# A one-core attention and feed-forward kernel: the one-hot product in two row strips, and half of x2 transposed by VectorE and moved by transfers

## The chip, the core and the metric

The kernel runs on one core of a Trainium2 chip. The core has TensorE (matrix products, two records each here: PEld loads the stationary operand, PE streams the moving one), VectorE (DVE), ScalarE (ACT), GpSimd (POOL), SyncE (SP, which here only issues transfers) and 16 DMA engines that carry out what SP and ACT issue. The metric is the device time of one execution in microseconds; lower is better.

## The reference, cut to what matters

All arithmetic is float32. `x` has 32 batches of 32 rows (channels) by 512 columns, 1024 rows in all.

```python
h  = einsum('bct,bcd->bdt', x, cond_weights[itok])     # 16 matrices of 32x32, one chosen for each batch
q, k, v = h @ Wq + bq, h @ Wk + bk, h @ Wv + bv        # 512 -> 4096, 32 heads of 128; rms_norm of q and k
x2 = x + softmax(q k^T / sqrt(128)) v @ Wo + bo        # attention inside each batch of 32 rows
y  = causal_conv(x2, K) + D * x2, columns >= length masked   # one filter K of 512 taps for each channel
out = x2 + y @ ffn_w + ffn_b + (low-rank terms chosen by a gate)
```

The first line is called the mix below, `x2` is the residual stream after attention, and the fourth line is the convolution.

## The kernel before, in words

The program is one straight list of instructions for each engine; semaphores order them against each other. The order of each list is written out by hand. The 1024 rows are eight groups of 128 rows (four batches of 32). There are four stretches.

**Start (0 to 17 us).** Which of the 16 matrices a batch uses is a one-hot product on TensorE: `onehot` (16 rows that count, the other 112 hold zeros in `cond_nat`) times `cond_nat`, twice 512 columns (L825). VectorE fills the unused rows of `cond_nat` with zeros (L1526, L1527), builds `onehot` (L1533, L1536), and turns the product from PSUM into the block-diagonal `mix_w` in two transposes (L1549). `spin` (L817) is a run of products whose result nobody reads; it stands ahead of the one-hot product and behind it. Then come eight groups of the mix (L839, order MIX_ORDER = 0, 4, 1, 5, 2, 3, 6, 7), which ScalarE and VectorE carry out of PSUM as a high part, a low part and a whole (`mix_hi`, `mix_lo`, `mix_f`). SP loads x in four pieces of two groups each, and the weights of head 0 (`w_raw`) behind the first two pieces.

**Heads and values (17 to 506 us).** Products for 32 heads, then for the values. GpSimd forms sums of weights and of `mix_f` for them, one behind the other, starting with L520.

**Attention and output projection (506 to 744 us).** Eight units; each multiplies into four PSUM banks and VectorE adds these to `acc` (L1840), which becomes x2. Units 6 and 7 finish the groups 0 to 3 and 4 to 7 of x2. In unit 7, TensorE does `project_first(7)`, then the transposes of the finished groups 0 to 3 (`transpose_x2`, L1119, four of 128x128 each), and then `project_second(7, g)` for g = 0 to 3 with the transposes of groups 4 to 7 between and behind them. ScalarE copies each transposed group from PSUM to `x2p` (`x2_out`, L1484). `x2p` is stored as [partition, channel, chunk, batch], so that this copy writes with a stride of 128 elements and a stationary operand of the convolution is 32 elements in a row.

**Convolution and feed-forward (744 us to the end).** `convolve(u)` (L1149) for u = 0 to 7, each 16 products of 32 columns of `x2p` by a strip of `toep`, four of them side by side in the four column strips of the array. `toep0` is loaded by SP at about 723 us, once VectorE has turned `a_turn` and `b_turn` (L1877, L1878); behind it SP sends these through DRAM (`a_scr`, L456, 16 transfers; `b_scr`, L458, 4 transfers) and reads them back as `a_all`, `b_all` (L462 to L466), and loads `fb_rows` (L468). ScalarE needs `b_all` at L1504, in the fourth step of the convolution; TensorE needs `a_all` behind the last.

## Time and profile before

| | us |
|---|---|
| median of 3 runs | 806.17 (805.47 to 806.24) |
| the profiled execution's own time | 805.49 |
| its span | 803.7 |
| PE busy | 795.6 |
| DVE busy | 643.1 |
| POOL busy | 520.5 |
| ACT busy | 332.2 |

Busy time is the sum of an engine's instructions. The chain of waits is followed back from the last instruction to whatever released each step. A timeline row gives the start, the time that the row's instructions span, engine, line, operation, tiles and how many instructions are merged; in brackets stands how long the engine had been idle and what released it. SPq and ACTq are rows of issued transfers. A row by stretch gives the stretch, its length, busy time and count of PE, PEld, DVE, ACT and POOL, the granted clock (1.00 is full), the mean busy share of the 16 DMA engines, and GB/s. A product in float32 shows as two PE records for each matmul.

### The profile page before, as it was taken

The numbers are of one execution on the slowest core, as the hardware profiler recorded it, in microseconds if no ns is written. First come the engines' busy times: TensorE is split into PE (matmuls) and PEld (weight loads), VectorE is DVE, ScalarE is ACT, GpSimd is POOL, SyncE is SP. The second block draws the span as 40 slices with busy tenths as digits, with TensorE's granted clock in tenths as the row PEclk, the third lists the DMA queues.
The fourth block names the chain that finished last, engine by engine and source line by source line (L and its number), as shares of the span: only waits on it lengthen the run. The fifth ranks groups of instructions, "written<-read, shape, count | busy, mean of one in ns | idle before, by whom it ended". The sixth has DMA issues, their size and how long they took to land.

```text
span 803.7 us, 15196 instructions
## 1 busy us (share of the span) xinstructions
PE 795.6 (99%) x6093; PEld 651.7 (81%) x6093; DVE 643.1 (80%) x646; ACT 332.2 (41%) x374; POOL 520.5 (65%) x451
## 2 busy tenths in 40 slices
PE   9999999999999999999999999999999999999998
PEld 7777888888888888888888888888888888888466
DVE  7799888888888888987889769989899888861442
ACT  4655555555555555572222226322422331322520
POOL 4999887333333333428998995979999999910420
PEclk9999999999999999999999999999999999999999
DMA  7031111111111111304434421456404813418502
GB/s 207 28 85 50 52 52 52 53 52 52 52 52 52 52 52 42 115 2 157 182 139 180 180 105 55 169 79 187 157 1 157 316 61 147 157 50 257 127 18 88
DMA packets 80735, 81.87 MB, mean 102 GB/s; under 512 B 26044, under 2 KB 61212, under 8 KB 78652
## 3 DMA queue, kind: packets, MB, share of 16 engines
q1 hardware_dynamic: 80188, 81.24, 31.2%
q8 instruction: 25, 0.41, 0.2%
q10 hardware_dynamic: 512, 0.13, 0.1%
q14 instruction: 10, 0.08, 0.0%
HBM read 64.97 MB, written 16.40 MB: 101 GB/s over the span
## 4 chain that ended last, share of the span: by engine, by line
PE 91%; DVE 3%; POOL 3%; ACT 2%; DMA 1%; issue 1%; SPq 0%; DVEq 0%; POOLq 0%
PE psum L862 13%; PE psum L864 12%; PE psum L863 12%; PE psum L808 7%; PE psum L810 7%; PE psum L809 7%; PE psum L1061 7%; PE psum L1090 4%; PE psum L1092 4%; PE psum L1091 4%; PE psum L1078 3%; PE psum L1080 3%; PE psum L1079 3%; PE psum L901 3%; PE psum L1149 1%; DMA w_raw<-in_wk 1%
## 5 line engine op out<-in xcount | busy, mean ns | idle before, releaser
L506 POOL TENSOR_TENSOR w_raw<-w_raw 128x256 f32<-128x256 f32 x31 | 45.1, 1454 | 123.1 <-DMA w_raw<-in_wk 122.6
L862 PE MATMUL psum<-t_hi,w_hi 128*128 128x512 f32 x248 | 100.5, 405 | 0.0
L864 PE MATMUL psum<-t_hi,w_lo 128*128 128x512 f32 x248 | 96.5, 389 | 0.0
L863 PE MATMUL psum<-t_lo,w_hi 128*128 128x512 f32 x248 | 96.5, 389 | 0.0
L1370 ACT ACTIVATE sq<-qk_sb 128x1024 f32<-128x1024 f32 x31 | 32.9, 1063 | 140.7 <-issue 127.5
L1637 DVE TENSOR_TENSOR sumsq<-sumsq,sq 128x1024 f32<-128x1024 f32 x62 | 80.2, 1295 | 0.0
L1409 ACT ACTIVATE at_hi<-psum,params 128x512 fp32r<-128x512 f32 x64 | 44.0, 688 | 69.6 <-PE psum L1061 69.6
L862 PE MATMUL psum<-mix_hi,w_hi 128*128 128x512 f32 x186 | 72.5, 390 | 0.2 <-DVE w_lo L1541 0.2
L863 PE MATMUL psum<-mix_lo,w_hi 128*128 128x512 f32 x186 | 72.4, 389 | 0.0
L864 PE MATMUL psum<-mix_hi,w_lo 128*128 128x512 f32 x186 | 72.4, 389 | 0.0
L1541 DVE TENSOR_TENSOR w_lo<-w_raw,w_hi 128x1792 fp32r<-128x1792 f32 x30 | 61.4, 2047 | 1.5 <-ACT w_hi L1246 1.5
L1061 PEld LDWEIGHTS psum<-p_blocks,v_sb 128*128 128x128 f32 x512 | 58.5, 192 | 0.7
L1061 PE MATMUL psum<-p_blocks,v_sb 128*128 128x128 f32 x512 | 58.6, 275 | 0.0
L1826 DVE SCALAR_TENSOR_TENSOR at_lo<-psum,params,at_hi 128x512 fp32r<-128x512 f32 x64 | 47.2, 748 | 11.4 <-ACT at_hi L1409 5.0
L862 PEld LDWEIGHTS psum<-t_hi,w_hi 128*128 128x128 f32 x248 | 46.5, 187 | 10.6 <-DVE qk_sb L1629 1.1
L864 PEld LDWEIGHTS psum<-t_hi,w_lo 128*128 128x128 f32 x248 | 46.5, 188 | 10.1
L863 PEld LDWEIGHTS psum<-t_lo,w_hi 128*128 128x128 f32 x248 | 46.6, 188 | 8.3
L1246 ACT ACTIVATE w_hi<-w_raw 128x1792 fp32r<-128x1792 f32 (+2 forms) x32 | 52.8, 1651 | 1.1 <-POOL w_raw L511 1.0
L1078 PE MATMUL psum<-wo_hi_a,at_hi 128*128 128x512 f32 x128 | 50.5, 395 | 1.0 <-DVE wo_lo_a L1796 1.0
L1090 PE MATMUL psum<-wo_hi_b,at_hi 128*128 128x512 f32 x128 | 50.3, 393 | 0.1
L1080 PE MATMUL psum<-wo_hi_a,at_lo 128*128 128x512 f32 x128 | 49.9, 389 | 0.0
L1092 PE MATMUL psum<-wo_hi_b,at_lo 128*128 128x512 f32 x128 | 49.8, 389 | 0.0
(287 smaller groups left out, 2130.2 us busy)
## 6 DMA issues: line engine op xcount, KB each, us to landing
v_sb<-v_scr_dram SPq DMA_DIRECT2D x6, 2048.0 KB, 7.9
v_scr_dram<-v_sb SPq DMA_DIRECT2D x9, 1024.0 KB, 3.9
w_raw<-in_wq SPq DMA_DIRECT2D x32, 256.0 KB, 2.9
w_raw<-in_wk SPq DMA_DIRECT2D x32, 256.0 KB, 3.2
wv_raw<-in_wv SPq DMA_DIRECT2D x16, 512.0 KB, 4.4
toep<-kpad_dram SPq DMA_DIRECT2D x2, 4096.0 KB, 14.5
wo_raw_a<-in_wo SPq DMA_DIRECT2D x4, 1024.0 KB, 5.2
wo_raw_b<-in_wo SPq DMA_DIRECT2D x4, 1024.0 KB, 5.2
```

The costliest lines, as they stand in the source:

```text
L808: mm(out, lh, rh, start=(fresh and n == 0), stop=False)
L809: mm(out, lh, rl, start=False, stop=False)
L862: mm(bank(n), wh, hi[:, c, tok], start=(i == 0), stop=False)
L863: mm(bank(n), wh, lo[:, c, tok], start=False, stop=False)
L864: last = mm(bank(n), wl, hi[:, c, tok], start=False, stop=(i == 1))
L1061: last = mm(bank(PV_BANK[u % 4])[:, P * g:P * g + P], v_sb[:, part, g, cols], p_blocks[:, u, g, :], start=True, stop=True)
L1078: mm(bank(O_BANK[g]), at_hi[:, h, tok], wo_hi_a[:, h, :], start=(h == 0), stop=False)
L1080: last = mm(bank(O_BANK[g]), at_lo[:, h, tok], wo_hi_a[:, h, :], start=False, stop=False)
L1090: mm(bank(O_BANK[g]), at_hi[:, QUAD + h, tok], wo_hi_b[:, h, :], start=False, stop=False)
L1092: last = mm(bank(O_BANK[g]), at_lo[:, QUAD + h, tok], wo_hi_b[:, h, :], start=False, stop=(h == QUAD - 1))
L1541: v.tensor_tensor(w_lo[slot][:].rearrange("p b n -> p (b n)"), w_raw[slot][:, 1:8, :].rearrange("p b n -> p (b n)"), w_hi[slot][:].rearran ...
L1637: v.tensor_tensor(sumsq[:, m, :], sumsq[:, m, :], sq[:, m, :], ALU.add).then_inc(total, 1)
```

## The change

The start and the end of the program change; the long middle does not.

1. **One-hot product in two row strips.** `cond_nat` is now 512 columns wide: the first half of the 16 matrices' entries lies in partitions 0 to 15 and the second half in partitions 64 to 79, `onehot` exists in both places (`cond_i` is loaded to all partitions, and 64 is taken from the partition numbers of the upper half). The two products use only those 16 rows each, at the row positions 0 and 64 of the array, into two banks. The zero fills of VectorE go. Both transposes into `mix_w` wait for both products. `spin` has 7 products ahead and 5 behind, where it had 5 and 3.
2. **Load order and order of the mix's copies.** x groups are loaded as pairs (0, 2), (4, 6), (1, 3), (5, 7) of the table GROUP_AT, and the weights of head 0 are loaded behind the first pair, not behind the second. `x_nat` and later `acc` hold the groups in that order. VectorE's `mix_f` copy of group 4 is behind the `mix_lo` of group 5.
3. **Half of x2 without TensorE.** The four groups that unit 6 finished are turned by VectorE in 32x32 blocks into `x2_turn`, and ACT issues 16 transfers that bring the blocks to other partitions in `x2p`. Each is a quadrant of 32 partitions to another with 16 runs of 32 elements a partition (128 bytes a run, 64 KB a transfer), and the convolution waits for all of them (`x2_moved`). TensorE transposes only the four groups of unit 7.
4. **The last group in halves.** The last add to `acc`, the last transposes and the last `x2_out` are each split into two halves of 256 columns; `spin` behind has 2 products, not 5.
5. **Another layout of `x2p`:** [partition, chunk, group, batch, channel]. `x2_out` writes 128 elements in a row, and a stationary operand of the convolution is 32 elements with a stride of 32.

```diff
@@ start, TensorE @@
             pe.wait_ge(const_ok, 1)
-            spin(5, ones[:, :], 7)
+            spin(7, ones[:, :], 7)
             pe.wait_ge(cond_in, 48)
             pe.wait_ge(hot_ok, 1)
-            pe.wait_ge(fill_ok, 2)
-            for n in range(2):
-                mm(bank(n), onehot[:].rearrange("n q b -> n (q b)"),
-                   cond_nat[:].rearrange("n (c d) -> n c d", d=32)[:, :, 16 * n:16 * n + 16],
-                   start=True, stop=True).then_inc(mixw_mm, 1)
-            spin(3, ones[:, :], 7)
+            for i in range(2):
+                rows = slice(64 * i, 64 * i + NCOND)
+                last = mm(bank(i), onehot[rows].rearrange("n q b -> n (q b)"), cond_nat[rows, :],
+                          start=True, stop=True, tile_position=(64 * i, 0))
+            last.then_inc(mixw_mm, 1)
+            spin(5, ones[:, :], 7)
@@ start, SP @@
-            for n in range(2):
-                sp.dma_start(cond_nat[NCOND * n:NCOND * n + NCOND], cond_w.rearrange("n c d -> n (c d)")).then_inc(cond_in, 16)
+            for i in range(2):
+                sp.dma_start(cond_nat[64 * i:64 * i + NCOND], cond_cols[i]).then_inc(cond_in, 16)
             load_x(0)
-            load_x(2)
             load_qk(0, 0)
-            load_x(1)
-            load_x(3)
+            for n in (2, 1, 3):
+                load_x(n)
             load_qk(1, 1)
@@ start, VectorE @@
-            v.memset(cond_nat[64:P], 0.0).then_inc(fill_ok, 1)
-            v.memset(cond_nat[32:64], 0.0).then_inc(fill_ok, 1)
+            dve.wait_ge(sel_const, 1)
+            v.tensor_scalar(cond_no[64:P], cond_no[64:P], -64.0, None, ALU.add).then_inc(row_ok, 1)
...
             dve.wait_ge(blank_ok, 1)
+            dve.wait_ge(mixw_mm, 1)
             for n in range(2):
-                dve.wait_ge(mixw_mm, n + 1)
@@ unit 7, TensorE @@
             attend(7)
             project_first(7)
             pe.wait_ge(alo_ok, OCT * 8)
-            for g in range(4):
-                transpose_x2(g)
             project_second(7, 0)
...
             project_second(7, 3)
+            pe.wait_ge(acc_ok, HG * 7 + 3)
             transpose_x2(6)
-            transpose_x2(7)
+            pe.wait_ge(acc_ok, HG * 7 + 4)
+            transpose_x2(7, range(0, 2))
+            pe.wait_ge(acc_ok, HG * 7 + 5)
+            pe.wait_ge(x2p_ok, 1)
+            transpose_x2(7, range(2, 4), PV_BANK[0])
...
-            spin(5, ident[:, :], 7)
-            pe.wait_ge(x2p_ok, G)
+            spin(2, ident[:, :], 7)
+            pe.wait_ge(x2_moved, 16 * BPG * KC)
+            pe.wait_ge(x2p_ok, HG + 1)
             convolve(0)
@@ convolution, the stationary operand @@
-   mm(bank(2 + u % 2)[quadrant(q), P * c:FEAT], x2p[:, ch, c, :],
+   mm(bank(2 + u % 2)[quadrant(q), P * c:FEAT], x2p[:, c, :, :, ch].rearrange("p g b -> p (g b)"),
@@ unit 7, ScalarE @@
-            for g in range(G):
-                x2_out(g)
+            act.wait_ge(x2_turned, HG)
+            for b in range(BPG):
+                for k in range(KC):
+                    act.dma_start(x2p[quadrant(k)].rearrange("p c (g e) b s -> p e b (c g) s", e=2)[:, 0, b],
+                                  x2_turn[quadrant(b), k].rearrange("p c g s -> p (c g) s")).then_inc(x2_moved, 16)
...
+            for n in range(1, 4):
+                x2_out(n, n + 3)
+            x2_out(4, 7, slice(0, 2))
+            x2_out(5, 7, slice(2, 4), PV_BANK[0])
             act.wait_ge(ffn_in, 16)
@@ unit 7, VectorE, behind a_turn and b_turn @@
+                    dve.wait_ge(acc_ok, HG * 7)
+                    for g in range(HG):
+                        v.transpose(x2_turn[:, :, :, g, :].rearrange("p k c s -> p c k s"),
+                                    acc[:, g, :].rearrange("p (c k f) -> p c k f", c=KC, k=KC)).then_inc(x2_turned, 1)
                 accumulate(n, (0, 1))
...
-                accumulate(n, (2, 3))
+                accumulate(n, (2, 3) if n < 7 else (2,))
+            for half in range(2):
+                cols = slice(256 * half, 256 * half + 256)
...
+                v.tensor_tensor(acc[:, 7, cols], bank(O_BANK[3])[:, cols], acc[:, 7, cols], ALU.add).then_inc(acc_ok, 1)
```

TensorE's list at the end of `project_first(7)`, before; L1119 are the transposes of x2 (`acc` times `ident`):

```order
L1079 MATMUL psum<-wo_lo_a,at_hi 128x512
L1080 MATMUL psum<-wo_hi_a,at_lo 128x512
L1119 MATMUL psum<-ident,acc 128x128 x16
L1090 MATMUL psum<-wo_hi_b,at_hi 128x512
L1091 MATMUL psum<-wo_lo_b,at_hi 128x512
L1092 MATMUL psum<-wo_hi_b,at_lo 128x512
```

and now, where the same place has none of them:

```order
L1085 MATMUL psum<-wo_lo_a,at_hi 128x512
L1086 MATMUL psum<-wo_hi_a,at_lo 128x512
L1096 MATMUL psum<-wo_hi_b,at_hi 128x512
L1097 MATMUL psum<-wo_lo_b,at_hi 128x512
L1098 MATMUL psum<-wo_hi_b,at_lo 128x512
```

The sixteen transposes of the finished groups are gone between the two halves of the projection.

TensorE's list at the end of `project_second(7, 3)`, before; L817 is `spin`, L1149 the convolution:

```order
L1091 MATMUL psum<-wo_lo_b,at_hi 128x512
L1092 MATMUL psum<-wo_hi_b,at_lo 128x512
L1119 MATMUL psum<-ident,acc 128x128 x8
L817 MATMUL psum<-ident 128x128 x5
L1149 MATMUL psum<-toep,x2p 32x512 x4
L1149 MATMUL psum<-toep,x2p 32x384 x4
L1149 MATMUL psum<-toep,x2p 32x256 x4
```

and now (L1123, L823 and L1158 are the same three things):

```order
L1097 MATMUL psum<-wo_lo_b,at_hi 128x512
L1098 MATMUL psum<-wo_hi_b,at_lo 128x512
L1123 MATMUL psum<-ident,acc 128x128 x8
L823 MATMUL psum<-ident 128x128 x2
L1158 MATMUL psum<-toep,x2p 32x512 x4
L1158 MATMUL psum<-toep,x2p 32x384 x4
L1158 MATMUL psum<-toep,x2p 32x256 x4
```

The eight transposes of the two last groups stay, and three of the five spin products go.

ScalarE's list between the last attention output (`at_hi`) and the feed-forward weights, before:

```order
L1417 ACTIVATE wo_hi_b<-wo_raw_b 128x2048
L1409 ACTIVATE at_hi<-psum,params 128x512 x8
L1484 ACTIVATE x2p<-psum 128x4x4x32 x8
L1490 ACTIVATE ffn_hi<-ffn_raw 128x2048
L1497 ACTIVATE y_hi<-psum 128x128x4
```

and now, where `x_turn` is the tile that the code calls `x2_turn`:

```order
L1427 ACTIVATE wo_hi_b<-wo_raw_b 128x2048
L1419 ACTIVATE at_hi<-psum,params 128x512 x8
L1494 DMA x2p<-x_turn 32x16x32 x16
L1500 ACTIVATE x2p<-psum 128x4x128 x3
L1500 ACTIVATE x2p<-psum 128x2x128 x2
L1508 ACTIVATE ffn_hi<-ffn_raw 128x2048
L1515 ACTIVATE y_hi<-psum 128x128x4
```

Sixteen issues stand ahead of the first copy from PSUM, and the copies are three whole ones and two halves.

## Rows read from the trace of the kernel before

**Rows 1.** busy time and granted clock, from the page
```profile
PE 795.6 (99%) x6093; PEld 651.7 (81%) x6093; DVE 643.1 (80%) x646; ACT 332.2 (41%) x374; POOL 520.5 (65%) x451
...
PEclk9999999999999999999999999999999999999999
```

**Rows 2.** waits of TensorE: total, times, longest
```profile
PE psum L839 <- DVE mix_w L1549: 0.3, 1, 0.3
PE psum L862 <- DVE w_lo L1541: 0.2, 1, 0.2
```

**Rows 3.** the chain of waits of the first 18 us: start, length, what
```profile
3.14 5.76 DMA w_raw<-in_wk
...
12.53 0.74 POOL mix_f L520
```

**Rows 4.** timeline of TensorE, 0 to 10 us
```profile
0.99 2.50 PE L817 MATMUL psum<-ones 128*128 128x128 f32 x10 [0.99 <-POOL ones L482]
4.12 3.75 PE L825 MATMUL psum<-cond_nat,onehot 128*128 128x512 f32 x4 [0.62 <-DVE onehot L1536]
7.66 1.07 PE L817 MATMUL psum<-ones 128*128 128x128 f32 x6
9.02 1.16 PE L839 MATMUL psum<-mix_w,x_nat 128*128 128x128 f32 x8 [0.30 <-DVE mix_w L1549]
```

**Rows 5.** timeline of VectorE, 0 to 13 us
```profile
7.91 1.06 DVE L1549 STREAM_TRANSPOSE mix_w<-psum 128x512 f32<-128x512 f32 x1 [0.60 <-PE psum L825]
```

**Rows 6.** timeline of ScalarE, the first copy of the mix, and b_hi
```profile
10.22 0.60 ACT L1256 ACTIVATE mix_hi<-psum 128x512 fp32r<-128x512 f32 x1 [0.23 <-PE psum L839]
...
761.26 1.91 ACT L1504 ACTIVATE b_hi<-b_all 128x2048 fp32r<-128x2048 f32 x1
```

**Rows 7.** the chain of waits, 740 to 752 us
```profile
744.20 2.07 ACT x2p L1484 x2
```

**Rows 8.** timeline of TensorE, 725 to 775 us
```profile
729.96 1.91 PE L1119 MATMUL psum<-ident,acc 128*128 128x128 f32 x16
...
744.51 0.66 PE L1119 MATMUL psum<-ident,acc 128*128 128x128 f32 x4 [0.35 <-DVE acc L1840]
745.01 1.28 PE L817 MATMUL psum<-ident 128*128 128x128 f32 x10
746.33 4.51 PE L1149 MATMUL psum<-toep,x2p 128*32 128x512 f32 x64
```

**Rows 9.** timeline of VectorE, 720 to 750 us
```profile
721.80 1.20 DVE L1878 STREAM_TRANSPOSE b_turn<-b_sum 128x1024 f32<-128x1024 f32 x1
...
743.77 0.69 DVE L1840 TENSOR_TENSOR acc<-psum,acc 128x512 f32<-128x512 f32 x1 [2.50 <-PE psum L1092]
```

**Rows 10.** tile a_scr_dram: issue time ns, min/median/max, first and last issue
```profile
L456 SPq DMA_DIRECT2D a_scr_dram<-a_turn x16: 450/458/4189, 723.4 to 739.0; - x16
```

**Rows 11.** busy time by stretch; last columns granted clock, DMA share, GB/s
```profile
723.00:730.00 7.00, 7.00 (x33) 5.74 (x32) 0.00 (x1) 0.00 (x0) 0.00 (x0) 1.00 0.94 337
730.00:736.00 6.00, 6.00 (x36) 5.27 (x35) 0.69 (x1) 3.82 (x4) 0.00 (x0) 1.00 1.08 364
736.00:739.50 3.50, 3.50 (x19) 2.87 (x18) 0.69 (x1) 1.09 (x1) 0.00 (x0) 1.00 0.58 88
739.50:745.00 5.50, 5.15 (x29) 4.15 (x28) 1.38 (x2) 1.89 (x2) 1.09 (x2) 1.00 0.71 110
```

**Rows 12.** transfer queues, 2 to 10 us: packets, MB, share
```profile
q1 hardware_dynamic: 2021, 2.37, 91.7%
q10 hardware_dynamic: 428, 0.12, 7.0%
```

**Rows 13.** tile expo: strided stationary loads, ns min/median/max, first and last start
```profile
L1101 PEld LDWEIGHTS psum<-expo,prod x64: 104/114/121, 531.2 to 532.1; 128*16 128x16 f32 x64
```

**Rows 14.** tile b_all: its last issue, and its landing
```profile
L466 SPq DMA_DIRECT2D b_all<-b_scr_dram x2: 556/576/597, 746.7 to 748.1; - x2
...
DMA to landing us min/median/max: 6.0/7.1/8.0
```

More of the change, by code:

```diff
@@ L282, in build_program @@
         out_rows = out.rearrange("(g p) f -> g p f", p=P)
+        cond_cols = [cond_w.rearrange("n c d -> n (c d)")[:, 512 * i:512 * i + 512] for i in range(2)]
         wqk_cols = [w.rearrange("(c p) n -> p c n", p=P) for w in (wq, wk)]
@@ L1111, in _, with transpose_x2 @@
                         kern()
-            def transpose_x2(g):
-                pe.wait_ge(acc_ok, HG * 6 + g + 1)
-                if g >= 4:
-                    pe.wait_ge(x2p_ok, g - 3)
-                for c in range(KC):
-                    last = nc.tensor.transpose(bank(PV_BANK[g % 4])[:, P * c:P * c + P], acc[:, g, P * c:P * c + P], ident[:, :])
+            def transpose_x2(g, part=range(KC), to=None):
+                for c in part:
+                    last = nc.tensor.transpose(bank(PV_BANK[g % 4] if to is None else to)[:, P * c:P * c + P], acc[:, g, P * c:P * c + P], ident[:, :])
                 last.then_inc(xt_mm, 1)
@@ L1564, in mix_out, with mix_whole @@
                 v.tensor_tensor(mix_lo[:, :, tok], src, mix_hi[:, :, tok].bitcast(F32), ALU.subtract).then_inc(mixlo_ok, 1)
-                if n not in MIXF_ACT:
-                    v.tensor_copy(mix_f[:, :, tok], src).then_inc(mixf_ok, 1)
+            def mix_whole(n):
+                tok = slice(P * MIX_ORDER[n], P * MIX_ORDER[n] + P)
+                v.tensor_copy(mix_f[:, :, tok], bank(2 + n % 6).rearrange("p (c t) -> p c t", c=KC)).then_inc(mixf_ok, 1)
             dve.wait_ge(whi0_ok, 1)
@@ L1571, in _ @@
                             w_hi[0][:, 0:4, :].rearrange("p b n -> p (b n)").bitcast(F32), ALU.subtract).then_inc(wlo_ok, 1)
-            for n in range(G):
+            for n in (0, 2):
                 mix_out(n)
+                mix_whole(n)
+                mix_out(n + 1)
+            mix_out(4)
+            mix_out(5)
+            mix_whole(4)
+            mix_out(6)
+            mix_whole(6)
+            mix_out(7)
             b11, b12, b21, b22 = (mix_f[:, chunks, HALF * i + P * 3:HALF * i + P * 4]
```

49 lines of the change are left out of this document (30 added, 19 removed).

## The prediction, made before the changed kernel was run

> **What bounds the kernel now.** I read the page first: TensorE is busy for 795.6 of 803.7 us at the full granted clock [rows 1]. Time is therefore to be had only where TensorE's work shrinks, where it waits, or where what it does is filler. The waits of TensorE over the whole span are short, and two of them matter here: 0.3 us for `mix_w` and 0.2 us for `w_lo` at 38.8 us [rows 2]. Filler shows in the timeline only: `spin` stands at 0.99, 7.66 and 745.01 us [rows 4, 8]. So the start lasts until the mix begins at 9.02 us, and the seam into the convolution until 746.33 us; both are set by chains outside TensorE. At the seam the chain of waits goes through two `x2_out` copies of ScalarE, 744.20 to 746.27 us [rows 7]; the spin, 745.01 to 746.29, ends at the same time [rows 8].
>
> **Start.** Before: one-hot product at 4.12 us, four PE records of 512 columns until 7.87 [rows 4]. The first starts at 4.12 and the spin behind them at 7.66, so a record paces at (7.66 − 4.12) / 4 = 0.88 us, and 512 columns in two passes at 1.2 GHz are 0.85 us: the array runs at the lower of its two levels here, although row 2 of the page prints full clock from the first slice. The ten spin records at 0.99 us agree, 0.25 us each, where 128-column records of the mix come every 1.16 / 8 = 0.145 us and those at 729.96 us every 1.91 / 16 = 0.12 us, the end of the last one included [rows 4, 8]. Ahead of the product TensorE stood idle for 0.62 us.
> Now: seven spin products are 14 records, 0.99 + 14 × 0.25 = 4.49 us. The product starts 0.4 us later than before, with no pause ahead of it, and if the two strips run side by side it takes 2 records, 1.7 us, plus some 0.2 of tail: 6.4 us if the clock is still low, 5.7 if it has risen by then, which the missing pause makes likelier. Two transposes of 1.06 us [rows 5] back to back: 7.8 to 8.5; I take 8.2. The mix begins 0.8 us earlier. If the strips run one behind the other it is 8.9 to 9.6, from 0.1 us earlier to 0.6 later.
> Is anything else late then? Head 0's weights landed at 8.90 us, 5.76 after their issue [rows 3]. They now have one x pair (1 MB / 2 = 0.5 MB) less ahead of them, at 2.37 MB in 8 us of rows 12 some 1.7 us, so they land near 7.3. x pair (4, 6) takes their place at about 9.0, and is wanted at 8.2 + 4 × 2 × 0.12 = 9.2. VectorE's and GpSimd's chain, whose first sum starts at 12.53 [rows 3], hung on these weights; the first mix copy of 0.60 us on ScalarE [rows 6] now starts near 9.2 instead of 10.22, and this chain moves forward by about 1.0 us. It released TensorE at 38.8 us 0.2 us too late [rows 2], and moves by more than TensorE, so that 0.2 goes too. The sum for the start is −1.0 us, range −1.6 to −0.2. Nothing until 730 us changes, and TensorE, nearly always busy, carries the gain through. The zero fills and the moved `mix_f` copy cost or save nothing further: VectorE is not awaited there.
>
> **Seam, TensorE's side** (times of the trace before, the gain of the start left aside). Sixteen transposes leave TensorE's list; they span 729.96 to 731.87 and delay the next product by 1.8 us [rows 8]. The last sum of x2 starts at 743.77 [rows 9], now at 742.0. Before, 2.56 us passed from there to the convolution. Now: the first half add, 0.4 us (half of 0.69 plus a start-up); the second half add, 0.35; two transposes, 0.3; the last half copy. The copy wrote 128x512 in 1.04 us with a stride (2.07 for two) [rows 7], while the mix's copy of the same size without one takes 0.60 [rows 6], so a half is 0.35. Sum 1.5 us, and the spin of four records ends no later. TensorE, VectorE and ScalarE alone would thus start the convolution at 743.6: −2.7 us.
>
> **Seam, the transfers' side.** VectorE ends `b_turn` at 723.0; 128x1024 took 1.20 us [rows 9], four of 128x512 take 2.4 to 2.8, so ACT issues from 725.6. An issue took 0.45 us at least, and up to 4.19 us where transfers were queued [rows 10]: 16 × 0.45 = 7.2 us is the least. The first data move about 726.9.
> Work: 16 × 512 = 8192 runs of 128 bytes. From 739.5 to 745 us only such runs moved (`b_turn`'s): 110 GB/s × 5.5 us / 128 B = 4,730 runs in 0.71 × 5.5 × 16 = 62.5 us of engine time, 13.2 ns each [rows 11]. So the new work is 8192 × 13.2 / 16 = 6.8 us of all 16 engines. Nothing here moves SBUF to SBUF in such runs, so 13.2 ns is taken from a write to DRAM.
> Room: from 723 to 745 us the shares 0.94, 1.08, 0.58, 0.71 [rows 11] are 6.6 + 6.5 + 2.0 + 3.9 = 19.0 us of work, and the engines are full until 736 (`toep0`). With 6.8 added all is done near 749.5. So everything depends on how the 16 engines share between ACT's queue and SP's.
> What the trace shows is the start: from 2 to 10 us both queues held work, and SP's got 2,021 packets against ACT's 428 [rows 12], per engine 126 and 27. ACT's were nine small transfers of 3 packets an engine; so ACT's queue came to its turn about nine times, a whole transfer's share each, between some 14 packets of SP's. If a turn stays a transfer's share, each of the 16 new ones (32 runs an engine) costs 0.42 us behind about 14 packets of `toep0`, 1.3 us by 337 GB/s [rows 11]. In the 9.1 us of `toep0` left, 7 go through, until 738.9; the other 9 alternate with shares of `a_scr` of 16 runs, (32 + 16) × 13.2 ns = 0.63 us each, until 744.6. With half a turn either way that is 743.6 to 745.5; I take the convolution's start as 744.5, that is −1.8 us against 746.33.
> ACT would be free of issuing some transfers earlier and do its copies (3 × 0.6 + 2 × 0.35 = 2.5 us) until then.
>
> The Trainium skill says in DMA: Bandwidth & Descriptors (section Queues, rings and completion order) that SP and ACT each have rings of their own on each engine, and that an engine alternates between them packet by packet, a packet being some 9 to 17 descriptors. By that, equal numbers would go through while both queues are full, and the sum would be the first rival's below. The start's 126 to 27 agrees with turns of about 14 but can't show what a turn holds for long transfers.
>
> **Behind the seam.** SP's `a_scr` and `b_scr` end near 749.5 instead of 745.9, so `b_all`, which landed by 748.1 + 8.0 = 756.1 [rows 14], comes by 759.9. ScalarE's `b_hi` wants it at 761.26 [rows 6], now at 759.5: +0.3 us. The convolution's stationary operand now has a stride of 32 elements. The filter product at 531 us loads such operands (16 columns, the same stride): 64 of them start within 0.9 us, 14 ns each [rows 13]. Twice the columns are 28 ns; the convolution has one each 4.51 / 64 = 70 ns [rows 8]. I take 0, with +1 us as the upper bound.
>
> **Sum.** −1.0 − 1.8 + 0.3 = −2.5 us against the profiled execution's 805.49, which gives 803.0; that execution lies 0.7 below the median of the runs, 806.17, and on their scale the sum is 803.7. I forecast 803.4. A measurement of this kernel tells about 0.2%, 1.6 us.
>
> **Rivals.**
> *Equal turns.* The two queues alternate in equal numbers of packets. For: rows 12 would look the same with small transfers. Then ACT has 100 of its 512 runs an engine through when `toep0` ends at 737, and needs as many runs of SP's beside the other 412: 412 × 2 × 13.2 ns = 10.9 us, until 747.7 with a slower SP allowed for. The convolution starts 1.4 us later than before, and with −1.0 the total is 0.4 above: 806.2, range 805 to 807.5.
> *The pause costs the clock (slower).* In the case just told TensorE has one spin's work between 743 and 747.7 us. At the start it ran at half its pace, after next to no work and a pause. If the granted clock falls in this pause, the first two convolution steps (4.51 us) and the turn take up to twice as long, +2 to +4.5 us: 808 to 811. It decides once the transfers end about 3 us after the transposes. Against: the last two transposes wait for ACT's first copy, which splits the pause.
> *Strided stationary loads bound the convolution (slower).* A contiguous pair of PE records costs 70 ns now. If a strided load of 32 columns held the array for 28 ns more, 256 × 28 ns = 7.2 us: 811. Rows 13 speak against it.
> The Trainium skill, SBUF — State Buffer (section Door 1: The DMA port swizzle, the note on cachelines), says that reads which leave their 16-byte line at each element pay a penalty. By that rule this rival would be right; the 14 ns per load of rows 13 contradict it for this use.
> *The strips don't overlap, or the start's gain is lost,* with the seam as forecast: 804.3 to 805.
>
> **How the numbers follow.** Chances: forecast 0.46 (own range 801.8 to 804.6); lost start 0.08; equal turns 0.30; lost clock 0.11; strided loads 0.05. Faster by over 0.2% (under 804.6): the forecast and part of the lost start, 0.49. Within: equal turns and the rest of the lost start, 0.35. Slower (over 807.8): 0.16. The range that leaves out 2 in 10 is 801.6 to 808.0.
>
> **What would show it.** The mix's first product at 8.2 us, not 9; the two one-hot products' records side by side, with no pause ahead of them. At the seam: whether the wait ahead of the first convolution product is for a transfer into `x2p` or for `x2p`'s last copy; where between 743 and 748 us (less 1.0) it starts; 13 ns for a run; and the stride, in whether two convolution steps still take 4.5 us. The forecast is wrong if the transfers land after 746 us, or if the convolution begins at the lower clock.

## The result and the profile after

The changed kernel takes 810.08 us (median of 5 runs, 809.96 to 810.92) where the kernel before takes 806.17 beside it: ratio 1.0052, 95% interval 1.0041 to 1.0063. It is slower by 3.9 us, about 0.5%; forecast were 2.8 us less. The profiled execution took 810.63 us with a span of 808.6, against 805.49 and 803.7: 4.9 us more.

TensorE over the start of the changed kernel, answering to [rows 4] (start, duration in us, line, what, count of records, idle before):

```profile
0.99 3.35 PE L823 MATMUL psum<-ones 128*128 128x128 f32 x14 [0.99 <-POOL ones L485]
5.35 2.08 PE L831 MATMUL psum<-cond_nat,onehot 16*128 16x512 f32 x4 [1.00 <-DVE onehot L1554]
7.35 2.50 PE L823 MATMUL psum<-ones 128*128 128x128 f32 x10
9.65 8.88 PE L845 MATMUL psum<-mix_w,x_nat 128*128 128x128 f32 x64
```

The two strips do run side by side: four records of 512 columns in 2.08 us, where [rows 4] have 3.75. But the product starts at 5.35, not 4.49, after a pause of 1.00 us, and the mix takes 8.88 us, not 7.41: its records come 6 or 7 in a us until about 13 us and 11 in a us behind, so the array stayed at its lower clock far into it. VectorE's cast, which stood at 3.49 us before, names the input that was late, the table in `cond_nat`:

```profile
4.68 0.20 DVE L1551 CAST cond_f<-cond_i 128x32 f32<-128x32 int32 x1 [3.30 <-DMA cond_nat<-in_cond_w]
...
7.53 1.97 DVE L1567 STREAM_TRANSPOSE mix_w<-psum 128x512 f32<-128x512 f32 x2 [2.33 <-PE psum L831]
...
724.34 2.45 DVE L1910 STREAM_TRANSPOSE x_turn<-acc 128x512 f32<-128x512 f32 x4
...
743.42 0.76 DVE L1922 TENSOR_TENSOR acc<-psum,acc 128x256 f32<-128x256 f32 x2 [2.50 <-PE psum L1098]
```

At the seam, TensorE and then ScalarE, answering to [rows 7, 8]:

```profile
743.22 1.12 PE L1123 MATMUL psum<-ident,acc 128*128 128x128 f32 x6
746.80 0.66 PE L1123 MATMUL psum<-ident,acc 128*128 128x128 f32 x2 [2.46 <-ACT x2p L1500]
747.25 1.06 PE L823 MATMUL psum<-ident 128*128 128x128 f32 x4
748.97 6.77 PE L1158 MATMUL psum<-toep,x2p 128*32 128x512 f32 x64 [0.66 <-DMA x2p<-x_turn]
```

```profile
726.83 19.18 ACTq L1494 DMA_DIRECT2D x2p<-x_turn  x16
746.06 2.13 ACT L1500 ACTIVATE x2p<-psum 128x512 f32<-128x512 f32 x5 [24.70 <-issue]
```

ScalarE issues its sixteen transfers until 746.0 us and copies nothing before. TensorE's last two transposes need the bank that the first copy frees. They wait 2.46 us, and then the convolution waits 0.66 us for the transfers. By stretch (columns as in [rows 11]; PEclk is the one ahead of the DMA share):

```profile
730.00:736.00 6.00, 6.00 (x28) 4.98 (x27) 0.69 (x1) 0.00 (x0) 0.00 (x0) 1.00 1.09 375
736.00:739.50 3.50, 3.50 (x19) 2.90 (x18) 0.69 (x1) 0.00 (x0) 0.00 (x0) 1.00 1.28 259
739.50:745.00 5.50, 4.75 (x25) 3.56 (x24) 1.45 (x3) 0.00 (x0) 1.44 (x2) 1.00 0.98 145
745.00:750.00 5.00, 2.54 (x14) 1.65 (x18) 0.00 (x0) 3.93 (x6) 0.69 (x1) 0.67 0.93 139
750.00:755.00 5.00, 5.00 (x52) 2.02 (x48) 2.98 (x2) 0.00 (x0) 0.00 (x0) 0.64 0.63 232
```

The granted clock is full until 745 us and its mean is 0.67 and 0.64 in the next two stretches of 5 us: it went to half after the pause, and the first 64 records of the convolution took 6.77 us instead of 4.51 [rows 8].

The account of the profiled execution closes:

- `a_turn` starts at 722.06 instead of 720.64 us: +1.42, what is left there of a mix that ended 2.1 us later;
- from there to the convolution it takes 26.91 us instead of 25.69: +1.22;
- the first two steps of the convolution: +2.26;
- all behind them: 52.86 us in both.

Together this is 4.90. It is one execution of each kernel, and how far single executions differ before the seam comes with e2.

### The profile page after: what moved, and what is told of

Its sections match the earlier page's. It is cut to its first block, busy times and chain, and to the rows that moved or that the text cites. A ratio compares the mean times of both kernels' runs of the same rounds, so it can differ in the third digit from the quotient of the medians.

```text
span 808.6 us, 15181 instructions
## 1 busy us (share of the span) xinstructions
PE 798.2 (99%) x6079; PEld 656.2 (81%) x6079; DVE 643.0 (80%) x650; ACT 326.7 (40%) x371; POOL 521.0 (64%) x451
## 4 chain that ended last, share of the span: by engine, by line
PE 95%; ACTq 2%; DVE 1%; DMA 1%; ACT 0%; issue 0%; SPq 0%; DVEq 0%
PE psum L868 13%; PE psum L869 12%; PE psum L870 12%; PE psum L814 7%; PE psum L815 7%; PE psum L816 7%; PE psum L1067 7%; PE psum L1084 3%; PE psum L1096 3%; PE psum L1085 3%; PE psum L1097 3%; PE psum L1086 3%; PE psum L1098 3%; PE psum L907 3%; PE psum L1158 3%; ACTq L1494 2%
## 5 line engine op out<-in xcount | busy, mean ns | idle before, releaser
L1855 DVE SCALAR_TENSOR_TENSOR at_lo<-psum,params,at_hi 128x512 fp32r<-128x512 f32 x64 | 47.2, 748 | 11.4 <-ACT at_hi L1419 5.0
L1085 PE MATMUL psum<-wo_lo_a,at_hi 128*128 128x512 f32 x128 | 49.8, 389 | 0.0
```

The source lines that it names most:

```text
L1085: mm(bank(O_BANK[g]), at_hi[:, h, tok], wo_lo_a[:, h, :], start=False, stop=False)
```

## The experiments

Each set of timed runs had the kernel before beside it on the same chip. Its median lay between 805.70 and 806.55 us there, so ratios are compared. The expectations were written before each run.

**e1, e2: each half of the change alone.** e1 keeps the start of before (five spins, one product of 128 rows, x pairs in the old order) under the changed seam; e2 is the reverse.

Of e1 against the changed kernel, its core:

```diff
-            spin(7, ones[:, :], 7)
+            spin(5, ones[:, :], 7)
...
-                mm(bank(i), onehot[rows].rearrange("n q b -> n (q b)"), cond_nat[rows, :],
-                          start=True, stop=True, tile_position=(64 * i, 0))
+                mm(bank(n), onehot[:].rearrange("n q b -> n (q b)"),
+                   cond_nat[:].rearrange("n (c d) -> n c d", d=32)[:, :, 16 * n:16 * n + 16],
+                   start=True, stop=True).then_inc(mixw_mm, 1)
```

> The changed kernel with the start of the kernel before (one product of K = 128 rows over both copies of the table, five and three spins, two loads of x ahead of head 0's weights), and the changed seam. If the start costs 1.4 to 1.7 us by itself and the seam the rest, this takes 810.1 - 1.5 = 808.6 us, TensorE begins the convolution about 1.4 us earlier than in the changed kernel (747.5), and the granted clock still falls there. If the two are tied together (an earlier TensorE waits longer for the same transfers), the seam gives all of the 3.9 us: 809.5 to 810.

> The kernel before with the changed start alone. If the start is late because its inputs land late and the clock rises at 12.9 us instead of 8.1, this takes 806.2 + 1.5 = 807.7 us. If the start's loss is made up later (by the head start of head 0's weights), it takes 806.2 us. The forecast on record said 805.2.

e1: 809.82 us, ratio 1.0038 (1.0026 to 1.0050). e2: 806.23 us, 1.0001 (0.9986 to 1.0016). Most of the loss is the seam's. In e1 the last product of attention, at 741.53, and the transposes are 1.46 us earlier than in the changed kernel, and the convolution, at 747.71, is 1.26 earlier. So TensorE waits only 0.2 us of its lead away, and the first theory of e1 holds at the seam. Its time fits the second (809.5 to 810) for another reason: behind the convolution the profiled execution waits twice for `y_tok`, 1.1 us in all, and then the product of `a_all` takes 5.38 us, where it took 3.71 in both kernels. The waits at e1's seam (line, what for, us in total, times, longest):

```profile
PE psum L1123 <- ACT x2p L1500: 2.5, 1, 2.5
PE psum L1158 <- DMA x2p<-x_turn: 1.5, 1, 1.5
```

The changed start alone costs nothing that can be measured over twelve runs, although its trace has the same late product (5.23 us). The interval is wide, though: it reaches from 1.1 us less to 1.3 us more, and so leaves room for the start's forecast of −1.0.

The time of e2 fits the theory that the loss is made up later, but its trace shows another way than that theory tells. The mix ends 0.7 us later than before, and yet the last transposes start 0.15 us earlier (744.36). The lead comes from TensorE's wait for `wo_lo_a` at 514 us: 0.23 us here, 0.95 in the kernel before. That wait is short or long with either start (0.2 in e5, 0.9 in e11). Up to the seam e4 and e12 run the same instructions, and the same transposes start at 743.31 and 744.49. One execution can't tell what a start is worth to 1 us, and this holds for the +1.42 above too. The profiled execution of e2 took 807.72 us, above the median, since its clock fell behind the convolution, after two waits for `y_tok` of 0.65 and 0.54 us:

```profile
771.33 5.34 PE L1180 MATMUL psum<-y_t,a_all 128*64 128x128 f32 x64 [0.69 <-ACT y_t L1500]
```

**e3: work in the pause.** The changed kernel with

```diff
             pe.wait_ge(acc_ok, HG * 7 + 5)
+            spin(9, ident[:, :], 7)
             pe.wait_ge(x2p_ok, 1)
...
-            spin(2, ident[:, :], 7)
+            spin(6, ident[:, :], 7)
```

> The changed kernel with 9 spin products ahead of the wait for the first copy of x2p, and 6 instead of 2 behind the last transposes. If the clock falls because TensorE stands still for 2.46 us there, it stays at full speed now, the first two steps of the convolution take 4.6 us instead of 6.8, and the kernel takes 810.1 - 2.2 = 807.9 us. If the fall has another cause, it takes 810 us and the granted clock still falls at 746 to 747 us.

808.94 us, 1.0030 (1.0018 to 1.0042). TensorE at the seam:

```profile
742.25 2.27 PE L823 MATMUL psum<-ident 128*128 128x128 f32 x18
745.02 0.44 PE L1123 MATMUL psum<-ident,acc 128*128 128x128 f32 x2 [0.49 <-ACT x2p L1501]
745.29 1.50 PE L823 MATMUL psum<-ident 128*128 128x128 f32 x12
747.19 4.57 PE L1159 MATMUL psum<-toep,x2p 128*32 128x512 f32 x64 [0.39 <-DMA x2p<-x_turn]
```

The transposes still wait for ScalarE, but the first 64 records take 4.57 us and the clock stays up: the standstill made the clock fall, and that fall was 2.2 us. In time 0.0022 of the ratio came back, 1.8 us, and more than half of the loss remains. In this trace it is the transfers' lateness (the transposes of the last groups start at 741.24, 2.3 us earlier than before, and the convolution 0.9 later) and once more the product of `a_all`, 5.38 us.

**e4: no transfers, all transposes on TensorE.** The kernel before with `x2p` laid out as changed, the last group in halves, two spins:

```diff
-                sc.activation(x2p[:, :, :, BPG * g:BPG * g + BPG].rearrange("p s c b -> p c b s"),
+                sc.activation(x2p[:, part, g, :, :],
...
-            transpose_x2(7)
+            transpose_x2(7, range(0, 2))
+            pe.wait_ge(acc_ok, HG * 7 + 5)
+            pe.wait_ge(x2p_ok, 5)
+            transpose_x2(7, range(2, 4), PV_BANK[0])
```

> The kernel before with the start and all sixteen transposes of x2's groups 0 to 3 left on TensorE as they are, but with x2p in the changed layout (contiguous copies, strided stationary loads) and the last group in halves, no transfer between partitions, two spins. If the copies are the seam's chain (1.04 us each with the stride, 0.6 without) and loads cost 0.03 us per 16 products, the convolution starts at 745.3 instead of 746.3, and the kernel takes 806.2 - 1.0 + 0.4 = 805.6 us (range 805.0 to 806.0). If the strided loads are what cost the changed kernel time beside the clock, it takes 806.5 or more.

805.84 us, 1.0000 (0.9987 to 1.0013). The convolution starts at 745.23, 1.1 us earlier than in [rows 8], and loses 0.06 us a step: 2.42 us for 32 records, 2.36 before. So the strided stationary loads cost about 0.5 us in eight steps. Of the 1.1 us, 0.26 are there before the last eight transposes start (743.31, 743.57 before); copies without a stride, the halves and the shorter spin bring the other 0.8. Its times don't resolve the difference.

**e5: what the three engines can do.** e1 without the transfers and ScalarE's issues. GpSimd fills their places with zeros, so the kernel leaves out half of x2 in the convolution:

```diff
+            pool.wait_ge(x2_turned, HG)
+            gp.memset(x2p[:, :, 0:G:2], 0.0).then_inc(x2_moved, 1)
             pool.wait_ge(wo_mm, HG * 8)
```

> The kernel e1 (start of the kernel before, changed seam) without the sixteen transfers: GpSimd fills the places of groups 0 to 3 in x2p with zeros, at about 727 us, so those groups' values are left out of the computation. VectorE's four transposes into x2_turn stay. This is the forecast's sum for the three engines by itself: if the transfers and their issue are all that is wrong with the seam, the last transposes wait for nothing, the convolution starts 2.2 to 2.4 us after the last product of attention (743.8; e1: 747.7), the granted clock stays up, and the kernel takes 806.0 - 2.4 + 0.5 (stride) = 804.1 us. If something else holds the seam (the halves, the copies), it takes 805.5 us or more.

804.70 us, 0.9981 (0.9972 to 0.9990), and

```profile
743.12 0.61 PE L825 MATMUL psum<-ident 128*128 128x128 f32 x4
743.80 4.57 PE L1160 MATMUL psum<-toep,x2p 128*32 128x512 f32 x64
```

The prediction's figure for the engines' side, 743.6, holds. The whole seam loss is the transfers': how they are issued and when they land.

**e6, e7: the transfers on SyncE.** e6 puts the loop of sixteen behind `toep0` on SyncE; e7 puts it between two halves of `toep0`:

```diff
-            sp.dma_start(toep0[:], bass.AP(kpad.tensor, 0, [[1, P], [PADL, 16], [1, 512]])).then_inc(toep_in0, 16)
+            sp.dma_start(toep0[:, 0:8, :], bass.AP(kpad.tensor, 0 * PADL, [[1, P], [PADL, 8], [1, 512]])).then_inc(toep_in0, 16)
+            sp.wait_ge(x2_turned, HG)
+            for b in range(BPG):
+                for k in range(KC):
+                    sp.dma_start(x2p[quadrant(k)].rearrange("p c (g e) b s -> p e b (c g) s", e=2)[:, 0, b],
+                                  x2_turn[quadrant(b), k].rearrange("p c g s -> p (c g) s")).then_inc(x2_moved, 16)
+            sp.dma_start(toep0[:, 8:16, :], bass.AP(kpad.tensor, 8 * PADL, [[1, P], [PADL, 8], [1, 512]])).then_inc(toep_in0b, 16)
```

> The kernel e1 with the sixteen transfers issued by SyncE, behind toep0 and ahead of a_scr and b_scr, instead of by ScalarE. One queue serves them in order: toep0 is through near 737 us, 8192 runs at 13.2 ns on 16 engines take 6.8 us, so they land near 744.5, and ScalarE copies x2p at once. Convolution from 744.5 to 745.5, clock up, 804.8 to 805.8 us. If it is the runs themselves that are slow (more than 13.2 ns when nothing alternates with them), they land after 746 us and the kernel takes 807 us or more.

> The kernel e6 with toep0 in two halves of 8 channels, and the sixteen transfers between them, so that they land near 739 us, ahead of the end of attention; the second half of toep0, wanted by the third step at about 749 us, lands near 744. If the transfers' place in the queue is all, the convolution starts at 743.8 as without transfers, and the kernel takes 804.1 us, up to 0.3 more where b_hi waits for b_all, which comes some 4 us later than before. If the work taken out of the queues' reach comes back as a wait of the third step or of b_hi, it takes 805.5 us or more.

817.11 us, 1.0144 (1.0128 to 1.0159), and 816.91 us, 1.0143 (1.0128 to 1.0159). Both expectations failed in the time, and both held at the seam: the convolution starts at 745.01 in e6 and at 743.66 in e7. What came instead, in e7, on TensorE and on ScalarE:

```profile
775.66 2.31 PE L1178 MATMUL psum<-ident,y_tok 128*128 128x128 f32 x8 [9.61 <-DVE y_tok L1933]
```

```profile
768.54 1.91 ACT L1525 ACTIVATE b_hi<-b_all 128x2048 fp32r<-128x2048 f32 x1 [9.60 <-DMA b_all<-b_scr_dram]
```

`b_hi` stands in ScalarE's order ahead of the fifth step's copies, so all of ScalarE, then VectorE, then TensorE waited for `b_all`. I had priced its delay at 0.3 us, as if the 6.8 us of work went through on full engines. `b_all` landed at 768.5 us, 12.4 later than the 756.1 of [rows 14]. All DMA engines in 40 slices of 739 to 745 us of e6, where only SyncE's queue has work:

```profile
DMA  2388606892388706882388607882388607887801
GB/s 40 52 145 138 101 5 118 138 141 36 50 143 137 104 11 113 140 138 37 59 144 138 94 13 120 139 136 31 63 143 143 87 15 122 140 134 114 127 5 33
```

The work comes in bursts with gaps between them: the share is 0.6 on average, where two queues together reached 0.98 in 739.5 to 745 us of the changed kernel. At 0.6 the 6.8 us of work take 11.4 us (an estimate), most of the 12.4. On SyncE's queue alone the share was higher with larger transfers: 0.43 with those of 32 KB (`a_scr`, 745 to 750 us of e6), 0.60 with 64 KB, 0.71 with 128 KB (`b_scr`, [rows 11]). What makes the gaps is not shown.

**e10, e11: the same without the wait for `b_all`.** e10 is e7 with

```diff
-                if u == 3:
-                    act.wait_ge(b_in, 64)
-                    sc.activation(b_hi[:].rearrange("p j n -> p (j n)"), b_all[:].rearrange("p j n -> p (j n)"),
...
+            act.wait_ge(b_in, 64)
+            sc.activation(b_hi[:].rearrange("p j n -> p (j n)"), b_all[:].rearrange("p j n -> p (j n)"),
```

(behind ScalarE's loop over u), `b_lo` likewise behind VectorE's `y_low(7)`, and `fb_rows` loaded ahead of `b_scr`. e11 also gives half of the transfers to ScalarE:

```diff
             sp.wait_ge(x2_turned, HG)
-            for b in range(BPG):
+            for b in range(2):
...
+            act.wait_ge(x2_turned, HG)
+            for b in range(2, BPG):
+                for k in range(KC):
+                    act.dma_start(x2p[quadrant(k)].rearrange("p c (g e) b s -> p e b (c g) s", e=2)[:, 0, b],
```

> The kernel e7 (all transfers on SyncE, toep0 in two halves) with b_hi moved behind the eight turns on ScalarE, b_lo behind the last y_lo on VectorE, and fb_rows loaded between a_scr and b_scr. e7 waited 9.6 us for b_all, which landed at 768.5; the moved b_hi wants it at about 771.8. If that one wait and the clock that fell in it are e7's whole loss, TensorE waits nowhere over 1 us behind the seam, the clock stays up, and the kernel takes 803.5 to 804.7 us (e5, without transfers, 804.7). If b_lo, 2.6 to 2.9 us ahead of ax_lo, becomes the next wait, it takes 805 to 807 us.

> The kernel e10 with the transfers of b = 2, 3 issued by ScalarE and those of b = 0, 1 by SyncE between the halves of toep0. If one queue of short runs is bound by its own issue (64 KB in 0.85 to 1.15 us) and two queues together fill the engines (share 0.45 and 0.95), the transfers and all behind them are through earlier than in e10, b_all lands near 762 instead of 768.5, and the time is e10's or up to 0.5 us better. If ScalarE's issues still stand behind toep0's packets, its first copy of x2p at 736 us comes late, as in the changed kernel, and the seam is later than e10's by 1 us or more.

804.47 us, 0.9974 (0.9965 to 0.9983), and 804.24 us, 0.9972 (0.9962 to 0.9981). With the three moved pieces the kernel is 1.7% faster than e7, and TensorE waits for nothing over 0.8 us behind the seam. So e7's loss was that wait and what it did to the clock (in e7 the product of `a_all` behind it, 64 records, took 5.32 us; 3.71 in the kernel before). In e11 ScalarE is free in time (its last issue ends at 734.0, its first copy starts at 736.68), and `b_hi` finds `b_all` there at 769.35, where e10's `b_hi` still waits 2.2 us, until 772.5, that nobody feels. Counted from the first issue of the sixteen transfers, `b_all` landed after at most 41.7 us in e11 and after 45.7 in e10:

```profile
726.06 7.98 ACTq L1503 DMA_DIRECT2D x2p<-x_turn  x8
736.68 0.60 ACT L1509 ACTIVATE x2p<-psum 128x512 f32<-128x512 f32 x1 [16.09 <-PE psum L1129]
769.35 1.93 ACT L1530 ACTIVATE b_hi<-b_all 128x2048 fp32r<-128x2048 f32 x1
```

The two don't differ in time.

**e12: `b_lo` late alone.** e4 with

```diff
-                if u == 5:
-                    dve.wait_ge(bhi_ok, 1)
...
             y_low(7)
+            dve.wait_ge(bhi_ok, 1)
+            v.tensor_tensor(b_lo[:].rearrange("p j n -> p (j n)"), b_all[:].rearrange("p j n -> p (j n)"),
```

> The kernel e4 (all transposes on TensorE, contiguous copies, last group in halves, start of the kernel before) with b_lo moved behind the last y_lo on VectorE. b_lo's 2.6 us stand ahead of the product of the seventh step, for which TensorE waits 0.4 to 1.2 us in all. If that wait goes and nothing takes its place, this takes 0.4 to 1.2 us less than e4: 804.7 to 805.4 us. If the wait only moves to ax_lo, it takes e4's 805.8 us.

805.19 us, 0.9981 (0.9972 to 0.9990). TensorE's waits for `y_tok` are 0.4 us in two pieces, as in e4's own trace (0.5 at once in that of before), so the trace of one execution shows no gain. The other executions show where one may lie. In the traces with `b_lo` late (e10 to e13) the last wait for `y_tok` is 0.2 us and the product of `a_all` takes 3.71 us. In e1, e2, e3 and e8, with `b_lo` in its old place, there are two waits of over 0.5 us, and the product takes 5.15 to 5.38 (e5 waited as long and kept the clock). And beside one another on one chip, the mean granted clock was 0.998 or less in 5 of 26 runs of the kernel before, which took 807.8 to 808.4 us, and in none of the 32 of e10, e11 and e12. So `b_lo` late probably spares the product a fall of the clock; no run tests this by itself.

The interval of e12, which has no transfers at all, overlaps those of e10 and e11 on the same chip. What the transfers are worth beyond the moved `b_lo` is therefore not shown; the medians differ by 0.7 to 1.0 us.

**e8, e9, e14, e15: the start.** e8 is e2 with whole rows of the table (4 KB) loaded into each strip; e9 is e2 with `cond_i` on 16 partitions of each strip. Of each the line that counts:

```diff
-                sp.dma_start(cond_nat[64 * i:64 * i + NCOND], cond_cols[i]).then_inc(cond_in, 16)
+                sp.dma_start(cond_nat[64 * i:64 * i + NCOND], cond_w.rearrange("n c d -> n (c d)")).then_inc(cond_in, 16)
```

```diff
-            act.dma_start(cond_i[:], every_partition(cond_idx, BATCH)).then_inc(cond_in, 16)
+            for i in range(2):
+                act.dma_start(cond_i[64 * i:64 * i + NCOND], every_partition(cond_idx, BATCH, NCOND)).then_inc(cond_in, 16)
```

> The kernel e2 (the kernel before with the changed start) with whole rows of the table (4 KB, 64 KB a transfer, as before) loaded into each strip, of which each product reads its half. If the pieces of 2 KB at a stride of 4 KB are what lands late, VectorE's cast of cond_i starts at 3.5 us as before (4.6 in e2) and the product at 4.5 us with nothing ahead of it. If cond_i on 128 partitions lands late, the cast still starts at 4.5 us or later.

> The kernel e2 (the kernel before with the changed start) with cond_i loaded to the 16 partitions of each strip only, by two transfers, and cast in two pieces, instead of to all 128 partitions. If the 128 short writes of cond_i hold up the table that is loaded beside them, the table lands near 3.5 us, the cast starts at 3.6 to 3.9 us and the product near 4.5 us. If the place of the table on partitions 64 to 79 or anything else is the cause, the cast still starts at 4.5 us or later.

One execution each: 810.36 and 806.67 us, too little to compare times. In e8 the cast is even later (5.08 us): the size of the pieces is not the cause. In e9:

```profile
0.99 3.36 PE L817 MATMUL psum<-ones 128*128 128x128 f32 x14 [0.99 <-POOL ones L482]
4.28 2.08 PE L825 MATMUL psum<-cond_nat,onehot 16*128 16x512 f32 x4
6.29 2.50 PE L817 MATMUL psum<-ones 128*128 128x128 f32 x10
8.58 9.14 PE L839 MATMUL psum<-mix_w,x_nat 128*128 128x128 f32 x64
```

The cast starts at 3.23, the product at 4.28 with no pause, the mix at 8.58. So the load of `cond_i` to all 128 partitions, 128 short packets in the way of the table, made the table late. `cond_i` itself was not late: in the changed kernel it landed at 3.2 us, the second half of the table at 4.6. In all, the cast starts at 4.56 to 5.08 us in the four traces with the wide `cond_i` and at 3.20 to 3.45 in the four with the narrow one. Yet the mix of e9 takes 9.14 us and ends later than in the kernel before. So I ran e9 again, timed (e14), and with both products in one strip of 16 rows, one after the other (e15):

```diff
-                last = mm(bank(i), onehot[rows].rearrange("n q b -> n (q b)"), cond_nat[rows, :],
-                          start=True, stop=True, tile_position=(64 * i, 0))
+                last = mm(bank(i), onehot[0:NCOND].rearrange("n q b -> n (q b)"),
+                          cond_nat[0:NCOND, 512 * i:512 * i + 512], start=True, stop=True)
```

> The kernel e9 again, timed. If its clock always rises near 12.4 us, its mix ends at 17.7 instead of 16.4 us and it takes 806.5 + 1.3 = 807.8 us on this scale of the kernel before (806.2 if its earlier mix is what counts).

> The kernel e9 with both products of the one-hot start in the same 16 partitions, one after the other, instead of side by side in two strips, and cond_i as in e9. The product takes 3.7 us instead of 2.1, the mix starts at 10.1 us. If the clock rises late in the changed start because the product keeps TensorE busy for 1.7 us less, it rises at 7.2 to 10.3 us here, as in the nine traces with the start of before. If it rises late because only 16 of 128 rows work, it rises at 12 us or later here too.

e14: 805.33 us, 0.9996 (0.9987 to 1.0005). The same instructions as e9, in another execution:

```profile
4.33 1.13 PE L825 MATMUL psum<-cond_nat,onehot 16*128 16x512 f32 x4
5.38 1.38 PE L817 MATMUL psum<-ones 128*128 128x128 f32 x10
7.55 1.16 PE L839 MATMUL psum<-mix_w,x_nat 128*128 128x128 f32 x8 [0.78 <-DVE mix_w L1552]
10.46 8.15 PE L839 MATMUL psum<-mix_w,x_nat 128*128 128x128 f32 x56 [1.75 <-DMA x_nat<-in_x]
```

Here the array was at full speed already for the product (1.13 us, 2.08 in e9), and the mix started at 7.55. Then it ran into the next thing: x pair (4, 6), moved behind head 0's weights, came 1.75 us late, and the clock fell again (granted 0.50 from 11 to 14 us). e15 (804.94 us, one execution) also had it up early: its two products, one after the other, took 1.98 us, and the mix started at 8.40 and took 7.41. Its expectation fell on both sides: the clock can rise early with 16 rows, and it rose before the product could have helped. Read from the pace of the records, the clock rose at 4 to 5 us in four traces with the changed start (e3, e13, e14, e15) and at 10 to 13 us in four (the changed kernel, e2, e8, e9); with the start of before, in nine traces, it rose always between 7 and 10.5. What decides between early and late is open.

**e13: the whole change with both mends.** The changed start with e9's `cond_i`, the seam of e11.

> The whole change (start and seam) with both mends: cond_i to the 16 partitions of each strip only (e9), and at the seam the transfers on two queues around a halved toep0, with b_hi, b_lo late and fb_rows early (e11). If the mended start is worth what its mix shows (8.6 instead of 9.0 us), this takes e11's 804.2 us less 0.4: 803.8. If the granted clock rises at 12.4 us again, as in e9's trace, the mix ends 1.3 us later than with the start of before, and this takes 805.2 to 805.6 us.

802.82 us, 0.9965 (0.9952 to 0.9979), 2.9 us less than the kernel before beside it. It is the lowest ratio of all, but its interval overlaps that of e11: what the mended start adds is not resolved. Its trace had the early clock, the mix at 7.45, and

```profile
9.11 6.52 PE L851 MATMUL psum<-mix_w,x_nat 128*128 128x128 f32 x56 [0.50 <-DMA x_nat<-in_x]
...
742.33 0.61 PE L829 MATMUL psum<-ident 128*128 128x128 f32 x4
743.01 4.58 PE L1166 MATMUL psum<-toep,x2p 128*32 128x512 f32 x64
```

## Why the prediction was wrong

The sum was −1.0 (start) −1.8 (seam) +0.3 (behind it) = −2.5 us, and the profiled executions differ by +4.9. Of the 7.4 us between them, 2.4 are the start's, 3.0 the convolution's start, 2.3 the clock, a term that the sum held at nothing, and 0.3 go back for what was feared behind the seam. On the scale of the runs the sum gave 803.7; the 803.4 that was forecast has no working of its own.

**Start, −1.0 forecast.** In the profiled execution it was +1.4, in time alone (e2) 0.0, with the interval given above. Right: the strips overlap (2.08 us at the lower clock; forecast 1.7 and a tail of 0.2), the weights land earlier (`w_hi` starts at 7.85 us, 8.93 before), and TensorE carries most of a shift of the start through (+2.1 at the end of the mix, +1.42 at 722 us). The step that failed is "the product starts 0.4 us later than before, with no pause ahead of it": it took the inputs as landing when they did before, though `cond_i` had grown from 16 partitions to 128, and the table behind it landed for a product at 5.35 us. e9 takes that away, and the product starts at 4.28. The second failure is "5.7 if it has risen by then, which the missing pause makes likelier": e9 had no pause and its clock rose among the latest three of all. The last is the pair (4, 6), said to land at 9.0 for 9.2: at 10.5 in e14, 9.1 in e13, both late once the mix is early.

**Seam, TensorE's side, −2.7.** Right: 743.6 forecast, 743.80 in e5, 743.66 in e7. The half adds took 0.76, the transposes on VectorE 2.45 (2.4 to 2.8 were reckoned). A little of this is luck: the four pieces of the sum add up to 1.4 us and not to the 1.5 written, which would give 743.4, and e5 took 1.77 us from the last sum's start at 742.03.

**Seam, transfers, convolution at 744.5.** The price of a run was right: in 739 to 743 us ScalarE's 3133 packets took 64.7% of 16 engines, 13.2 ns each. The step that failed is "if a turn stays a transfer's share", and with it the 744.5; the convolution started at 748.97. Packets of the two queues (q1 SyncE's, q10 ScalarE's) in 731 to 735, then in 735 to 739, then in 739 to 743 us:

```profile
q1 hardware_dynamic: 694, 1.42, 94.9%
q10 hardware_dynamic: 686, 0.09, 14.6%
...
q1 hardware_dynamic: 1874, 0.91, 82.5%
q10 hardware_dynamic: 1877, 0.23, 39.0%
...
q10 hardware_dynamic: 3133, 0.39, 64.7%
q1 hardware_dynamic: 2067, 0.25, 43.3%
```

From 731 to 739 us the turns are equal in packets: the first rival, which I gave 0.30. It put the convolution at 747.7; with the start's 1.42 that is 749.1, and 748.97 was measured. An agreement so close is partly luck. Until 731 us only 18 packets of ScalarE's went through, and behind 739, once `toep0` is through, the numbers are no longer equal: each queue then goes as fast as it does alone (in e6, on SyncE's queue alone, 3122 packets of these transfers in 739 to 743 us, and 2219 of `a_scr`'s in 745 to 749). The start's 126 to 27 packets [rows 12] had fitted both readings; I chose the one the long transfers contradict, against the rule quoted beside it. The Trainium skill, DMA: Bandwidth & Descriptors (section Queues, rings and completion order), has an engine alternate between the rings packet by packet; with that this trace agrees while `toep0` runs (694 to 686 and 1874 to 1877).

**The clock.** "The pause costs the clock" had 0.11, a price of +2 to +4.5 and a total of 808 to 811: it cost 2.26 us, e3 took it back, and the total was 810.1. This rival and equal turns together are what happened at the seam. The rival needed the transfers about 3 us late. It was decided sooner, since I let ScalarE copy while its queue was full ("ACT would be free of issuing some transfers earlier"): it was free at 746.0, and the copy that I thought would split the pause made it.

**Stride, 0 with +1 as bound.** 0.06 us a step, about 0.5 in all (e4, e5). The stationary load over the whole convolution, of before and of the changed kernel (ns, least, median, most):

```profile
L1149 PEld LDWEIGHTS psum<-toep,x2p x256: 106/110/110, 746.3 to 767.9; 128*32 128x32 f32 x128
```

```profile
L1158 PEld LDWEIGHTS psum<-toep,x2p x256: 147/167/218, 749.0 to 773.0; 128*32 128x32 f32 x128
```

A strided load does take longer: 57 ns more each would be 14.6 us in 256, of which all but 0.5 is hidden. The Trainium skill, SBUF — State Buffer (section Door 1: The DMA port swizzle, the note on cachelines), lets such reads pay a penalty; the trace agrees for the load (167 ns for 110) and not for the time.

**Behind the seam, +0.3.** Not felt in the changed kernel. e7 shows that this term was the most fragile of all: 9.6 us.

With the two terms that failed put right (inputs, sharing), the change is worth what was forecast of it: e13 is 0.35% faster, forecast was 0.34%. That is no confirmation: e13 also has `b_lo` and `b_hi` moved, `toep0` in halves and the transfers on two queues, and e12 shows that a part of the gain needs no transfers.

## What to carry to other kernels

When a transfer grows in partitions, reckon it as a new transfer in the way of its neighbours, however few bytes it has. Before an engine is given transfers to issue, ask what it must do while its queue is full, and put nothing on it that another engine's pause hangs on. Where two queues are full, share them by packets: short runs get few bytes against long ones. Ahead of a stretch of short runs on one queue, look for who waits behind them in another engine's order. And compare two traces of the same instructions before a difference of 1 us between two kernels is read as the change.

## What the runs showed of the hardware

- Behind the convolution the clock also fell in some executions and not in others, mostly after two short waits for `y_tok`: the product of `a_all` took 5.34 us in the trace of e2 (waits of 0.65 and 0.54) and 3.71 in that of e14 (one of 0.45).
- At the beginning of the same program TensorE's clock rose near 12.4 us in one execution and near 4 us in another (e9 and e14), and the mix ended at 17.7 or 18.6 us, by different ways. One profiled execution of a start tells little of its time.
- ScalarE needed 19.2 us to issue sixteen transfers of 64 KB beside a full queue of SyncE's; eight took 8.0 us in e11. SyncE needed 18.4 us for the same sixteen behind its own `toep0` in e6: the issuing engine is held either way.
- Transfers of 64 KB in 128-byte runs on one queue leave gaps between them (share 0.6, 3122 packets in 4 us); with a second queue of short runs beside it the share was 0.98, and 5200 packets went through in 4 us.
- A strided stationary load of 32 columns took 167 ns instead of 110, and cost 0.06 us in sixteen products.
